# Two transformer layers on one core: three steps of each group's first slots put at other places in the order

## What is computed

```python
def _layer(x, wqkv, qs, ksc, wo, lg, lb, w1, b1, w2, b2):   # x: (4, 1024, 256)
    h = shift_token(x)                       # second half of the columns comes from the token before
    qkv = h @ wqkv                           # 256 -> 3 * 512, 8 heads of 64
    q, k, v = to_heads(...)
    q = l2norm(q) * qs;  k = l2norm(k) * ksc
    q, k = rotary_xpos(q, k)
    o = local_attention(q, k, v)             # windows of 128 tokens: the own one and the one before
    x = x + o @ wo
    h = shift_token(x)
    mu = h.mean(-1, keepdims=True)
    var = h.var(-1, keepdims=True)
    h = (h - mu) / jnp.sqrt(var + 1e-05) * lg + lb
    h = h @ w1 + b1                          # 256 -> 2 * 682
    a, g = jnp.split(h, 2, axis=-1)
    h = a * jax.nn.gelu(g, approximate=False)
    x = x + h @ w2 + b2
    return x
for l in range(2):
    x = _layer(x, wqkv[l], ...)
```

## Time and profile before

| | |
|---|---|
| median of 3 runs | 2188.03 us (2183.95 to 2192.35) |
| profiled execution | 2188.08 us |
| span of its instructions | 2186.3 us |
| mean granted TensorE clock in it | 0.949 |
| PE / DVE / ACT / POOL busy | 85% / 70% / 54% / 45% |
| chain that ended last: PE, DVE, issue, ACT | 36%, 19%, 7%, 6% |
| PE, time lost in front of L1243 to DVE l_o_lo L1589 | 29.9 us, 16 times |
| PE, time lost in front of L1231 to DVE l_h_lo L1538 | 22.8 us, 16 times |

### The profile page before, as it was taken

One profiled execution on the slowest core, in us unless ns is written; L12 is line 12 of the kernel. 1 busy time (PEld: TensorE's weight loads), 2 busy tenths in 40 slices (PEclk: granted clock), 3 DMA queues, 4 the chain that ended last, 5 costly groups with the idle time before them and its releaser, 6 DMA issues.

```text
span 2186.3 us, 36482 instructions
## 1 busy us (share of the span) xinstructions
PE 1866.0 (85%) x12941; PEld 1402.0 (64%) x12941; DVE 1522.5 (70%) x3736; ACT 1185.1 (54%) x2717; POOL 985.3 (45%) x781
## 2 busy tenths in 40 slices
PE   5568999999975899898899988887898998988986
PEld 3444444444433677787777867676786777877776
DVE  2668888777756586775867758585675867758673
ACT  0545555544344655656556566564656556565562
POOL 0325454647464544444434444443544535444451
PEclk7669999999987899999999999999999999999998
DMA  4000000101222000000000001010101000010000
GB/s 143 25 27 27 1 25 10 51 16 51 78 63 78 12 22 17 20 15 21 19 17 21 19 21 52 28 54 24 33 18 31 28 22 25 18 30 28 24 18 22
DMA packets 83406, 68.58 MB, mean 31 GB/s; under 512 B 10852, under 2 KB 79508, under 8 KB 83224
## 3 DMA queue, kind: packets, MB, share of 16 engines
q1 hardware_dynamic: 83224, 66.25, 9.8%
HBM read 45.22 MB, written 16.81 MB: 28 GB/s over the span
## 4 chain that ended last, share of the span: by engine, by line
PE 36%; DVE 19%; issue 7%; ACT 6%; DMA 2%; POOL 1%; SPq 0%; DVEq 0%; ACTq 0%; POOLq 0%
PE bank_O L1243 4%; PE bank_T L1231 3%; PE bank_P L260 3%; PE bank_A L260 3%; ACT share_x L1381 3%; PE bank_A L262 3%; PE bank_A L261 3%; PE bank_P L261 3%; PE bank_A L1220 3%; PE bank_P L262 3%; DVE l_t L1561 3%; DVE share_x L1577 2%; DVE l_u_lo L1642 2%; PE bank_T L1210 2%; PE bank_T L260 2%
## 5 line engine op out<-in xcount | busy, mean ns | idle before, releaser
L1812 POOL TENSOR_TENSOR share_x<-share_x,l_rinv 128x512 f32<-128x512 f32 (+1 forms) x256 | 251.0, 1002 | 374.8 <-DVE l_rinv L1585 374.6
L1800 POOL TENSOR_TENSOR l_t<-share_qk,l_tab 128x512 f32<-128x512 f32 x128 | 175.8, 1397 | 315.5 <-DVE l_ss L1543 310.1
L1381 ACT ACTIVATE share_x<-share_x,l_nb 128x256 f32<-128x256 f32 (+1 forms) x512 | 248.0, 486 | 81.7 <-DVE l_nb L1577 81.5
L260 PE MATMUL bank_A<-l_f_hi,l_w_hi 128*114 128x256 f32 (+1 forms) x768 | 220.4, 287 | 5.9 <-DVE l_f_lo L1622 3.7
L1577 DVE CUSTOM_DVE_ANT_0 share_x<-bank_A,share_scr 128x256 f32<-128x256 f32 (+1 forms) x512 | 177.3, 401 | 57.3 <-PE bank_A L1220 57.1
L262 PE MATMUL bank_A<-l_f_hi,l_w_lo 128*114 128x256 f32 (+1 forms) x768 | 216.3, 282 | 0.0
L261 PE MATMUL bank_A<-l_f_lo,l_w_hi 128*114 128x256 f32 (+1 forms) x768 | 216.2, 282 | 0.0
L1231 PE MATMUL bank_T<-ident,share_x 128*128 128x128 f32 x960 | 147.8, 288 | 66.9 <-POOL share_x L1812 34.4
L645 ACT ACTIVATE pr<-ps_S 128x1024 f32<-128x1024 f32 x128 | 130.7, 1023 | 124.7 <-PE ps_S L539 124.0
L1642 DVE TENSOR_TENSOR l_u_lo<-l_up,l_u_hi 114x256 fp32r<-114x256 f32 (+1 forms) x192 | 196.1, 1028 | 0.1
L895 POOL TENSOR_TENSOR acc<-acc,pr 128x1024 f32<-128x1024 f32 x64 | 155.6, 2432 | 53.0 <-ACT pr L645 48.7
(11 more groups left out here) (269 smaller groups left out, 5132.6 us busy)
## 6 DMA issues: line engine op xcount, KB each, us to landing
l_xs<-x_layers SPq DMA_DIRECT2D x64, 128.0 KB, 2.5
share_x<-in_x SPq DMA_DIRECT2D x8, 512.0 KB, 3.8
base_rows<-share_x SPq DMA_DIRECT2D x16, 256.0 KB, 2.1
x_layers<-share_x SPq DMA_DIRECT2D x16, 256.0 KB, 2.1
l_xs<-x_layers SPq DMA_DIRECT2D x64, 64.0 KB, 2.2
x_layers<-l_yb SPq DMA_DIRECT2D x32, 128.0 KB, 1.8
share_m<-base_rows SPq DMA_DIRECT2D x32, 128.0 KB, 2.9
out<-l_yb SPq DMA_DIRECT2D x32, 128.0 KB, 1.7
```

The costliest lines, as they stand in the source:

```text
L260: pe.matmul(out, a_hi, b_hi, start=(start and k == 0), stop=False)
L1381: eng.activation(row, row, ACT.Exp, bias=nb[:, R % SS, e:e + 1], scale=-1.0, accum_out=rsum[:, R % SS, e:e + 1]).then_inc(ex_ready, 1)
L1800: eng.tensor_tensor(dst[:, :, :, lo:lo + H2], src[:, :, :, hi:hi + H2], table[:, :, 1, lo:lo + H2].unsqueeze(2).to_broadcast([P, 2, LH, H2 ...
L1812: eng.tensor_tensor(row, row, rinv[:, R % SS, :].unsqueeze(2).to_broadcast([P, 2, P * windows(n)]), ALU.mult).then_inc(pn_ready, 1)
```

## The change

The queues hold the same instructions before and after; only their order on TensorE, ScalarE and VectorE is another.

- TensorE: `h_transpose` of the next group's second unit goes from the end of slot 1 to slot 0, between `project` and `values`.
- ScalarE: its `h_out` goes from slot 1 to slot 0, behind the exponentials of rounds 12 and 13.
- VectorE: its `h_split` goes to slot 0, between `residual` and `moments`; `o_split` goes ahead of the two `inverse` of its slot, in slots 0 and 2 (in slot 4 there is no `inverse`); `deviation` goes from slot 1 to slot 2, behind `o_split` and the two `inverse` of rounds 14 and 15, and directly ahead of `layer_norm`.

In the last group there is no next one, so that only the VectorE part remains; the other 15 have all of it.

```diff
@@ TensorE
                         if k == 3:
                             x_transpose(first), x_transpose(first + 1)
+                        if k == 0 and ahead:
+                            h_transpose(following + 1)
                         if k < 4:
                             values(*head(first, r - 4)), values(*head(first, r - 3))
-                    if k in ((1, 4, 7) if g >= 0 else (4, 7)) and ahead:
+                    if k in (4, 7) and ahead:
                         h_transpose(following + 1 + k // 3)
@@ ScalarE
-                    if k in ((1, 4, 7) if g >= 0 else (4, 7)) and ahead:
+                    if (k in (4, 7) or k == 0 and g >= 0) and ahead:
                         h_out(following + 1 + k // 3)
@@ VectorE
                     if g >= 0:
+                        if k in (0, 2, 4):
+                            o_split(first + 1 + k // 2)
                         if k < 3:
                             inverse(*head(first, r - 2)), inverse(*head(first, r - 1))
-                        if k in (0, 2, 4):
-                            o_split(first + 1 + k // 2)
                         if k < 2:
                             minima(*head(first, r)), minima(*head(first, r + 1))
                         if k == 0:
                             residual(first + 1)
+                            if ahead:
+                                h_split(following + 1)
                             moments(first)
                         if k == 1:
-                            if ahead:
-                                h_split(following + 1)
                             moments(first + 1)
+                        if k == 2:
                             deviation(first // 2)
-                        if k == 2:
                             layer_norm(first // 2, rs)
```

## The result

| | before | changed |
|---|---|---|
| median (6 runs each) | 2187.74 us (2183.18 to 2192.35) | 2163.48 us (2156.62 to 2165.76) |
| ratio, with 95% interval | | 0.9886 (0.9865 to 0.9906) |
| profiled execution, span | 2188.08, 2186.3 us | 2162.62, 2160.8 us |
| mean granted TensorE clock | 0.949 | 0.953 |

What follows compares the result with a forecast made beforehand. TensorE sets the pace, except 3.20 us a group hanging on a chain through ScalarE and VectorE. 15 groups times 1.8 us plus about 2 in the last, 29 in all, off 2188.08 gives 2159 us; range 2149 to 2172.

Steps and rivals of the forecast that it cites:

- What bounds: Slots 0 to 3: TensorE sets the pace except 3.20 us a group, waiting for h_split (1.48) and o_split (1.72).
- Slot 0, round 11: Round 11 on TensorE would now wait for h_split in slot 0, costing 0.15 us a group.
- Rival D: Slower: round 11's new wait for h_split loses far more than 0.15 us a group; 2200 us, chance 0.05.
- Slot 2, the gain of 2.88 us at `values`: Values of rounds 12 and 13 start at 1675.45 instead of 1678.33 on group 10's clock.
- The hold of `deviation`: Slot 2: deviation's links stand still while GpSimd's products run, two taking about 1 us each; group gains 1.8, not 2.1.
- Rival A: Deviation's links slip between GpSimd's instructions in slot 2, 2.1 us won a group; 2154 us, chance 0.15.
- The group's gain: Slots 0 to 3: values of rounds 14 and 15 start 1.8 us earlier per group, between 1.6 and 2.1.
- The signs named: TensorE's total waits: h_split to 2-4 us, o_split to 4-8, products up some 9, layer_norm up 4-10.
- The last group: No h_transpose there; of its 4.1 us wait for o_split about 2 us are won.
- Rival C: TensorE's wait only moves from round 13 to 11, o_split late for another reason; gain 0-5, 2185 us, chance 0.05.
- Rival B: Later slots' VectorE chains take gain back, only some 0.8 us a group stays; 2175 us, chance 0.09.
- Nothing lost, nothing won: Slot 0: putting o_split ahead of the inverse of rounds 10 and 11 changes nothing, with 1.7 us of cover.

Runs made afterwards that it cites:

- e7: The e1 kernel with h_out and the third unit's o_out moved between exponentials, and o_split between the two inverse; 2137.25 us, ratio 0.9775.
- e5: The changed kernel with GpSimd's products of rounds 14 and 15 cut to 8 of 256 columns, a probe only; 2141.95 us, ratio 0.9802.
- e3: The kernel before with only deviation moved to slot 2, behind inverse and o_split; 2160.23 us, ratio 0.9882.
- e1: The changed kernel with o_split put back behind the two inverse; 2145.06 us, ratio 0.9807.
- h: The part moving h_transpose, h_out and h_split to slot 0; alone against the kernel before: 2150.47 us, ratio 0.9838.
- d: The part moving deviation to slot 2; alone against the kernel before: 2160.23 us, ratio 0.9882.
- o: The part putting o_split ahead of the two inverse; alone against the kernel before: 2201.11 us, ratio 1.0067.
- e4: The kernel before with only o_split put ahead of the two inverse in slots 0 and 2; 2201.11 us, ratio 1.0067.
- e8: The changed kernel with deviation put between o_split and the two inverse in slot 2; 2219.40 us, ratio 1.0158.

## Why the prediction was right, and where it was off

- **What bounds.** Right, but for a small misreading: the `h_split` wait stands in 15 groups and not in all 16. Both waits of the earlier trace rows were real, and where all that feeds them was on time (e7) the slots became shorter by their sum.
- **Slot 0, round 11.** Right in kind. It cost 0.28 us and not 0.15: `p_transpose` of rounds 10 and 11 to `scores` took 1.30 us (1653.15 to 1654.45), 1.02 before. In e7, with `h_out` between the exponentials, it is gone. `h_transpose` did not wait for its load. Rival D is out.
- **Slot 2, the gain of 2.88 us at `values`.** With the 14.50 us by which group 10 starts earlier added, `values` of rounds 12 and 13 start at 1675.60, forecast 1675.45; gain 2.73. They still wait 0.40 us for `o_split`; the forecast said 0.3, and its own times give only 0.17 (`qkv` at 1673.62, and 1.66 from there to where the wait begins).
- **The hold of `deviation`.** Right, and closer than the row it came from had to be: two links of 0.98 and 0.96 us, `layer_norm` 0.73 us. Rival A is out, and e5 shows the cause: of two runs that differ only in the length of GpSimd's products one has the slow links.
- **The group's gain.** 1.5 us against 1.8. Two terms were mis-sized. `o_split` started 0.15 us later than worked out (1674.85 on the old clock for 1674.70): 0.08 of it is the `qkv` copy on ScalarE behind the dearer round 11 (1671.72 for 1671.64), 0.07 is that `o_split` followed `o_out` by 0.67 and not 0.60; the chain and `layer_norm` (1679.55 for 1679.4) came late with it. And `x_transpose` started 0.56 us behind the start of `layer_norm`, at 1680.11, where 0.4 was allowed. `values` follow at 1680.77, forecast 1680.45. Fifteen times 0.3 is 4.5 us, about what the forecast was too low by.
- **The signs named.** L1231 for `l_h_lo` fell to 0.6, below the 2 to 4 named: round 11's delay doesn't show as a wait in this view. L1243 for `l_o_lo` 8.0, as said; L1231 for the products grew by 5.7 and not some 9 (round 15 waits 0.34 us, round 14's 0.11 is not named as a wait); L1258 for `layer_norm` grew by 5.5, as said.
- **The last group.** 2.1 us, forecast about 2, and that is luck. The forecast had the gain as waiting that goes away. The named waits went from 4.09 and 0.23 us to 1.64, 0.34 and 1.67, so only 0.7 us of waiting went. The other 1.4 is the same work of TensorE done faster: behind the 4.09 us it had run at a granted clock of 0.57 over 4 us, now it ran at 1.00. The forecast had no term for that.
- **Rival C** (the wait only moves, and `o_split` was late for another reason): out. With the chain alone out of its way (e3) the wait of `values` for `o_split` goes, and 1.66 us a group are won.
- **Rival B** (the gain comes back later): out. The measure's 24.2 us are nearly all of the 25.5, and `x_transpose` in slot 9 waits 1.00 us as before.
- **What the forecast missed.** It took the change as one and priced the sum. "Nothing lost, nothing won" was said of the swap in slot 0, and is right there; in slot 2 the swap was only counted as the way to bring `o_split` forward. But `o_split` waits there for `o_out`, and `inverse` in front of it doesn't delay it (e1). The swap delays `inverse`, GpSimd's products, round 15 and, by the lock, the chain. It costs 18 us of the 42 that the other two parts win.
- **The parts don't add.** h wins 36 us, d 26, both 42; o loses 15 alone, 10 to 12 beside h, 18 beside both, and beside d about 6 by the slots, which the ratios don't resolve. They lie on one chain of ScalarE, VectorE and GpSimd, and each opens a wait that another had covered.

## What to carry to other kernels

Put a queue's steps in the order in which their inputs arrive, and among those that could run at once first the one whose successor on another engine takes longest: an instruction of 0.2 us that starts 2 us of work elsewhere goes in front of one of 0.7 us that starts nothing (of this second half e4 is the plainest test: there both had their inputs, and the other order cost 0.73 us a group). Before a chain of short dependent VectorE instructions is moved, look at what GpSimd does at its new place. When several moves are made at once, take each one away again by itself: here one of three was against the other two, and the sum looked like a success.

## What the runs showed of the hardware

- A VectorE link of 0.17 us, started while a GpSimd product of 1.02 us runs, ends when that product ends: 0.96 to 1.04 us when it starts with the product, 0.56 (e3) and 0.30 us (e1) when less of it is left. With two products back to back two links were held in the changed kernel. A reciprocal (0.17 us) and `o_split` (0.69 us, one input in PSUM) were not held beside the products in e1. The two products took 2.04 us beside the links, as without; beside the longer `layer_norm` 2.09 (before) and 2.25 us (e8).
- A wait of TensorE of 4.09 us (last group before) was followed by 4 us at a granted clock of 0.57, waits of 2.4 to 2.7 us (e8) by 6 us that read 0.72, in group 10 by 5 us at 0.50; waits of 1.48 to 1.72 us by none below 1.00. In between it goes either way: before, behind a wait of 2.03 us 1733.90 to 1737.90 reads 0.57, behind one of 2.02 us 1550.70 to 1554.70 reads 1.00. In e8 a group took 1.0 to 2.3 us more than the wait itself had been forecast to cost.
